# Exponentials of a cross-attention kernel: subtract the maximum on GpSimd first, or take it as the activation's bias

## The reference, cut to what matters

```python
x = x + xattn(layernorm(x), ctx, ctx, mask, w_q, w_k, w_v, w_o, b_o)

def xattn(Q, K, V, mask, w_q, w_k, w_v, w_o, b_o):   # 32 heads of 16, 8 groups of k and v
    q = (Q @ w_q.T).reshape(B, S, G, HG, HD)
    k = (K @ w_k.T).reshape(B, S, G, HD)
    v = (V @ w_v.T).reshape(B, S, G, HD)
    scores = einsum("bnghd,bmgd->bnghm", q, k) / sqrt(HD)
    scores = where(mask == 0, -inf, scores)
    scores = where(causal, scores, -inf)
    attn = softmax(scores, axis=-1)
    return einsum("bnghm,bmgd->bnghd", attn, v).reshape(B, S, D) @ w_o.T + b_o
```

## Time and profile before

| | |
|---|---|
| median of 3 runs | 1392.12 us (1390.97 to 1394.84) |
| the profiled execution | 1392.23 us, span 1390.5 us |
| busy | PE 1340.8, DVE 819.9, ACT 606.6, POOL 513.0 us |
| one ordinary pass of cross-attention | some 42 us, PE busy for 41.71 |

### The profile page before, as it was taken

One profiled execution on the slowest core, in us unless ns is written; L12 is line 12 of the kernel. 1 busy time (PEld: TensorE's weight loads), 2 busy tenths in 40 slices (PEclk: granted clock), 3 DMA queues, 4 the chain that ended last, 5 costly groups with the idle time before them and its releaser, 6 DMA issues.

```text
span 1390.5 us, 23678 instructions
## 1 busy us (share of the span) xinstructions
PE 1340.8 (96%) x8180; PEld 1068.0 (77%) x8180; DVE 819.9 (59%) x2085; ACT 606.6 (44%) x1135; POOL 513.0 (37%) x485
## 2 busy tenths in 40 slices
PE   8999999999999999999999999999988999999994
PEld 6788888888888888888886777777766877766762
DVE  5888865333333333333467787788786586666661
ACT  4444441111111111111126777777786324777772
POOL 4555542202020202020427554446453112655552
PEclk9999999999999999999999999999999999999997
DMA  6000002010110101010100000000011924566553
GB/s 257 1 0 0 0 30 107 0 46 5 42 38 8 45 0 45 0 46 1 49 12 17 21 21 21 21 5 17 6 47 46 374 81 159 92 106 105 95 98 46
DMA packets 20533, 73.41 MB, mean 53 GB/s; under 512 B 2320, under 2 KB 3344, under 8 KB 18000
## 3 DMA queue, kind: packets, MB, share of 16 engines
q1 hardware_dynamic: 10256, 46.93, 9.3%
q0 software_dynamic: 10176, 25.17, 9.2%
HBM read 52.95 MB, written 19.14 MB: 52 GB/s over the span
## 4 chain that ended last, share of the span: by engine, by line
PE 86%; DVE 6%; ACT 4%; issue 2%; DMA 1%; POOL 1%; POOLq 0%; DVEq 0%; SPq 0%; ACTq 0%
PE ps L782 21%; PE ps L784 21%; PE ps L783 21%; PE ps L1030 5%; PE ps L1215 5%; PE ps L1022 2%; DVE den L1641 2%; ACT cols L1434 2%; PE ps L1054 2%; PE ps L1122 2%; PE ps L1048 1%; ACT cols L1422 1%; PE ps L1185 1%; PE ps L1143 1%; PE ps L1019 1%
## 5 line engine op out<-in xcount | busy, mean ns | idle before, releaser
L782 PE MATMUL ps<-feat,wsplit 128*128 128x512 f32 (+1 forms) x672 | 247.1, 368 | 3.2 <-PE ps L784 2.1
L784 PE MATMUL ps<-feat,wsplit 128*128 128x512 f32 (+1 forms) x672 | 244.6, 364 | 0.0
L783 PE MATMUL ps<-feat,wsplit 128*128 128x512 f32 (+1 forms) x672 | 244.5, 364 | 0.0
L1291 ACT ACTIVATE sg<-ps 128x512 f32<-128x512 f32 x64 | 38.3, 598 | 369.1 <-PE ps L784 369.0
L1561 DVE TENSOR_TENSOR m_f<-ps,sg 128x512 f32<-128x512 f32 x64 | 44.2, 691 | 245.4 <-ACT sg L1291 245.4
L542 POOL CAST wsplit<-wraw 128x3072 fp32r<-128x3072 f32 x9 | 24.8, 2755 | 399.3 <-PEq L970 386.7
L1829 DVE CUSTOM_DVE_ANT_0 cols<-ps,msk 128x256 f32<-128x256 f32 (+1 forms) x512 | 146.2, 353 | 27.7 <-PE ps L1022 16.3
L782 PEld LDWEIGHTS ps<-feat,wsplit 128*128 128x128 f32 x672 | 126.7, 189 | 26.4 <-issue 6.6
L1422 ACT COPY cols<-ps 128x512 f32<-128x512 f32 x192 | 111.6, 581 | 77.7 <-PE ps L1030 77.7
L784 PEld LDWEIGHTS ps<-feat,wsplit 128*128 128x128 f32 x672 | 126.6, 188 | 19.9
L783 PEld LDWEIGHTS ps<-feat,wsplit 128*128 128x128 f32 x672 | 126.7, 189 | 19.7
(11 more groups left out here) (281 smaller groups left out, 3014.5 us busy)
## 6 DMA issues: line engine op xcount, KB each, us to landing
wraw<-weights SPq DMA_DIRECT2D x11, 1536.0 KB, 6.5
rawx<-weights SPq DMA_DIRECT2D x8, 1536.0 KB, 16.1
ctx_raw<-ctx_t SPq DMA_DIRECT2D x8, 512.0 KB, 4.6
h_rows<-hd POOLq DMA_DIRECT2D x16, 256.0 KB, 4.4
out<-acc SPq DMA_DIRECT2D x4, 1024.0 KB, 4.7
qkv_raw<-weights SPq DMA_DIRECT2D x6, 512.0 KB, 7.5
acc<-x SPq DMA_DIRECT2D x1, 3072.0 KB, 17.5
acc<-x SPq DMA_DIRECT2D x2, 512.0 KB, 7.0
```

The lines of the kernel that those rows point to most:

```text
L782: nc.tensor.matmul(out_, w_hi, m_hi, start=first, stop=False)
L783: nc.tensor.matmul(out_, w_lo, m_hi, start=False, stop=False)
L784: return nc.tensor.matmul(out_, w_hi, m_lo, start=False, stop=last)
```

## The change

Units of the first two sets no longer go to GpSimd. ACT makes their exponentials as it does those of the other sets: one activation for each head, here four of 128 columns, with the maximum as bias and scale -1. It waits for DVE's maxima (`mx`) in place of GpSimd's semaphore (`sub`), which is gone. On GpSimd the two splits of the next batch's h stand one behind the other.

```diff
-            def less_max(b, u):
-                pool.wait_ge(c["mx"], UNITS * b + u + 1)
-                s_u = sc[:, u % PLACES, :].rearrange("p (n k) -> p n k", n=4)
-                m_u = mxs[:, u % PLACES, :].rearrange("p (n o) -> p n o", o=1).broadcast_to([P, 4, P])
-                nc.gpsimd.tensor_tensor(out=s_u, in0=m_u, in1=s_u, op=ALU.subtract).then_inc(c["sub"], 1)
-
...
             for b in range(BATCH):
-                for u in range(4):
-                    less_max(b, u)
                 if b + 1 < BATCH:
-                    hT_split(b + 1, 0)
-                for u in range(4, 8):
-                    less_max(b, u)
-                if b + 1 < BATCH:
-                    hT_split(b + 1, 1)
+                    for t in range(TPB):
+                        hT_split(b + 1, t)
...
             def exps(b, u):
                 count, w = blocks_of(u)
                 s_u = sc[:, u % PLACES, :]
-                if u // 4 < FIRST_SETS:
-                    act.wait_ge(c["sub"], 4 * FIRST_SETS * b + u + 1)
-                    nc.scalar.activation(s_u, s_u, ACT.Exp).then_inc(c["P"], 1)
-                    return
                 act.wait_ge(c["mx"], UNITS * b + u + 1)
                 for n in range(count):
                     part = s_u[:, n * w:(n + 1) * w]
```

More of the change, by code:

```diff
@@ L393, in decoder_layer @@
             o_rawT="tiles of o, feature-major", oT_hi="the last one's hi", oT="tiles of o split", wo_ps="tiles of the output projection in PSUM",
-            S="sets with scores in PSUM", mx="units with masked scores and their maximum", sub="units less their maximum", P="units of probabilities",
+            S="sets with scores in PSUM", mx="units with masked scores and their maximum", P="units of probabilities",
             PT_ps="units transposed in PSUM", O="sets summed over v",
```

## The result

The changed kernel takes 1397.67 us (median of 7 runs, 1396.50 to 1398.87), the kernel before in the same rounds 1392.39 us (1390.97 to 1394.84): ratio 1.0037, 95% interval 1.0025 to 1.0048, that is 3.5 to 6.7 us more. The forecast was 1397.6 us, 5.5 us more. The profiled execution of the changed kernel is the slowest of its seven (1398.87 us, span 1396.8), so that the spans of the two profiles lie 6.3 us apart, a microsecond more than the medians.

A forecast was written before the change was run, and what follows sets the result against it. PE was taken to bound the kernel. Seven batches at +0.54 us (3.8 us) and the last batch's 1.7 us gave 5.5 us on 1392.1, so 1397.6 us; range 1393.5 to 1404.5 us.

The forecast's parts named there:

- Rival A: Short activations on ACT have a floor of 405 ns, giving 1417 us; chance 0.13 together with a milder floor.
- the milder one: A lower floor for the short activation, 320 to 350 ns, costing 9 to 15 us; chance 0.09.
- The cover rival: ACT's idle time hides the added work, the end lying within 4.2 us of before; chance 0.29.
- piece 9: PE's work amid eight transposes in an ordinary batch; said to wait 0.4 us for ACT's copy of piece 7.
- piece 10: PE's next piece after piece 9; said to wait 0.1 us more and start 0.54 us late each batch.
- the signs: What the profile should show if right, among them PE's new waits of about 0.4 and 0.1 us, once a batch.
- Pieces 4, 5 and hT1: PE's earlier work in an ordinary batch, around h's transposes; slacks of 0.27 and 0.17 us, so nothing lost.
- fall of the clock: PE at half clock for 3.4 us; more waits in the last batch could shift or add one, 1.7 us either way.
- piece 13: PE's work amid eight transposes in the last batch; said to start 1.7 us late, needing ACT's copy of piece 11.
- The bound of no change: About 0.3%, 4.2 us, is what a measurement can tell from no change; slower 0.68, same 0.29, faster 0.03.

The follow-up runs named there:

- c1_one: The changed kernel with one activation of 512 columns with a bias operand in place of the four, leaving out the maximum; ratio to before 0.9996.
- c5_five: The changed kernel with five activations a unit (128, 128, 128, 64 and 64 columns) in place of four; ratio to before 1.0085.
- last_new: The kernel before with the change made for the last batch alone; ratio to before 1.0018.
- u5_early: The changed kernel with unit 5's four activations moved ahead of one copy on ACT, same work; ratio to before 1.0026.

## Why the prediction was right

**The frame.** PE sets the time and GpSimd's is worth nothing: c1_one, with GpSimd out of it, is at 0.9996.

**The price of an activation.** 298 ns from start to start was estimated, 295 measured; 404 ns busy where about 400 were expected. The bias operand was inferred at 84 ns; c1_one shows it, 731 ns for 512 columns with it against 638 without, 93 ns (its scale differs as well, a constant in both). The Trainium skill (ScalarE: Activation LUTs, What ACT_TABLE_LOAD costs) has about 93 ns for a pointer operand, and the estimate of 294 ns from it was one off the measured 295: the trace agrees. Rival A, the floor of 405 ns or the milder one of 320 to 350, is excluded by the 295 ns, and 64 columns in c5_five take still less: (1.37 - 3 x 0.295) / 2 = 0.243 us. The cover rival needed 215 ns.

**An ordinary batch.** +0.54 predicted, +0.49 measured, at the places named: piece 9 came 0.42 late (0.4 predicted), piece 10 0.56 (0.54). The agreement is a little better than the working: by its own terms the prediction's piece 10 is 871.51 + 0.03 - 871.03 = 0.51 late, and the batches would give 3.6 us in place of 3.8; the signal from ACT's copy to PE took 0.10 us and not 0.03 (873.35 to 873.45), and 0.07 of the delay came back later in the pass. Of the two new waits of the signs only that at piece 9 is named in the profile, as 0.27 us of idle time; piece 10 shows in its start alone. Pieces 4, 5 and hT1 did not stall; at 1.37 us a unit hT1 did. ACT's busy time in one pass rose by 4.8 us (35.52 in 42.29 against 30.76 in 41.80), 0.5 less than the 5.3 forecast; the runs do not show why.

**The first batch.** Counted as an ordinary one; without a fall of the clock it is, +0.48 and +0.52 in two profiles. That ACT starts a microsecond earlier was worth nothing, as predicted: its wait there is 5.4 us for DVE in place of 6.5 for GpSimd, and PE waits the same 2.1 us for DVE's maxima.

**The last batch.** +1.7 predicted, +1.83 measured in last_new, 1.74 of it at piece 13, the piece named. In the changed kernel's own profiles it was +3.0 and +2.8, because the clock fell in it both times. I had put that in the range as up to 1.7 us either way and not into the sum. By the passes without a fall the sum is 7 x 0.49 + 1.83 = 5.3 us, and the medians differ by 5.3. That these meet is in part luck: the falls cost a microsecond or two wherever they come (in the last pass of both profiles of the changed kernel, behind the last pass in that of before), and what they did to the runs in the mean is not settled by one or two profiles of a kernel. The sign that "ACT has no gap from 1025 to 1045" failed in the changed kernel's profile: a gap of 1.04 us stands before the copy at 1036.54, where ACT waited for the slowed PE.

**The bound of no change.** Slower by over 0.3% had 0.68. The ratio is 1.0037 with an interval from 1.0025, so the time is slower than before beyond doubt, and by over 0.3% only likely.

## What to carry to other kernels

An engine with a quarter of its time free still has stretches without any: add up its work between two moments at which the bounding engine releases it, and put the new work where the idle time is. Here 38 us more on ACT cost 5 us in one order and nothing measurable in another, and one copy moved ahead of two activations gave 2.5 us. Count a split instruction's fixed part (some 190 ns of the 295 here, 128 columns being 107 by the earlier trace rows) as many times as it is issued, and read an effect of 0.3% from the periods of a repeated stage, which agree within 0.07 us in each profile, not from total times: those of one kernel scatter here by 2 to 7 us.

## What the runs showed of the hardware

The 3.4 us at TensorE's lower clock (1.2 GHz, a granted 0.5) come at places that change from one execution of the same kernel to the next: the changed kernel's first pass took 39.30 us with a fall and 37.98 without. A fall costs 1.3 us there (and 1.4 where the first pass is that of before: 38.86 in last_new, 37.50 in before) and 1.0 to 1.2 in the last pass (38.01 and 37.81 in the changed kernel, 36.83 in last_new without). All falls in the passes came within a microsecond behind a long wait of PE. In all thirteen profiles PE waits 2.10 us for DVE's maxima in the first pass; in eight of them the clock fell there, in five it stayed up. The last passes of five profiles have a wait of 2.0 to 2.2 us for ACT; in three the clock fell (both profiles of the changed kernel, u5_early), in two it did not (last_new, c5_five), and it fell in none of the eight whose longest wait there is 1.8 us or less. Ahead of the fall at 1065 in the kernel before, PE was busy for 4.82 of 8 us. A wait of 2 us thus went with a fall more often than not, and did not decide it. What does was not tried.

An activation of 64, 128, 256 and 512 columns with the bias operand lasts 350, 404, 510 and 731 ns here.
